# At the end of a turn px is added ahead of the gate and half a key unit follows the first turned rows; in the last turn unit 5 precedes the turned rows

## What is computed

```python
x = x + _L0_xattn_ref(ctx_1024, _layernorm(x), ...)   # selective scan over ctx, gated by silu of the normed x
x = x + _L0_ffn_ref(_layernorm(x), w1, w2)            # ternary-weight FFN, activations rounded to 8 bits
x = x + _L1_xattn_ref(_layernorm(x), ctx_1024, ...)   # cross attention, 16 heads, rms-normed q and k
x = x + _L1_ffn_ref(_layernorm(x), ...)               # mixture of 8 experts, top 2, and a shared one
```

```python
y = y + D[None, :, None] * u
y = y * jax.nn.silu(z)                                 # the gate
...
h = bitlinear(x, w1); h = new_gelu(h); h = bitlinear(h, w2)
...
k = rmsnorm((encoder_hidden_states @ Wk).reshape(B, Skv, H, D), gk)
return out.reshape(B, Sq, H * D) @ Wo
```

## Time and profile before

| | us |
|---|---|
| median of 3 runs | 1937.62 |
| lowest, highest | 1936.42, 1937.79 |
| profiled execution | 1934.49 |
| its span in the trace | 1932.8 |
| PE, DVE, ACT, POOL busy | 1797.8, 1206.4, 1090.6, 236.1 |

### The profile page before, as it was taken

How to read it: one execution, slowest core, us unless ns; L and a number is a source line. 1 busy time by engine, 2 the same in 40 slices (tenths; PEclk the granted TensorE clock), 3 DMA queues, 4 the chain that set the end, 5 groups by cost and what they waited for, 6 DMA issues and landing times.

```text
span 1932.8 us, 26062 instructions
## 1 busy us (share of the span) xinstructions
PE 1797.8 (93%) x8318; PEld 1154.4 (60%) x8319; DVE 1206.4 (62%) x1551; ACT 1090.6 (56%) x2454; POOL 236.1 (12%) x197
## 2 busy tenths in 40 slices
PE   7799899999999999999999999998989999989895
PEld 3455455776765576767655777765567676634442
DVE  5799778877775788777678977783641001144422
ACT  5577447666654676666547666754554554453420
POOL 0002011110100010000102000000031010033032
PEclk9799899999999989999999999999999999999997
DMA  7165222323231122223122323232044323213433
GB/s 213 44 191 189 88 57 66 93 76 94 83 84 61 51 87 89 91 77 102 50 88 66 93 76 103 76 120 77 33 137 90 78 68 85 49 50 108 127 105 124
DMA packets 113862, 175.76 MB, mean 91 GB/s; under 512 B 12400, under 2 KB 65648, under 8 KB 113280
## 3 DMA queue, kind: packets, MB, share of 16 engines
q1 hardware_dynamic: 99136, 158.06, 26.0%
q0 software_dynamic: 13840, 15.21, 3.9%
q10 hardware_dynamic: 816, 1.57, 0.2%
HBM read 146.23 MB, written 34.87 MB: 94 GB/s over the span
## 4 chain that ended last, share of the span: by engine, by line
PE 78%; DVE 9%; ACT 6%; issue 4%; another core or an unknown queue 2%; DMA 1%; POOL 1%; SPq 1%; ACTq 0%; DVEq 0%
PE ps L1942 27%; PE pp L1942 17%; PE px L1942 17%; PE pd L1942 6%; PE po L1942 5%; DVE arena L1469 2%; PE ps L2136 1%; PE pp L2290 1%; DVE arena L1461 1%; ACT hbuf L1235 1%; PE pd L2261 1%; PE po L2261 1%; ACT arena L980 1%; PE px L1994 1%
## 5 line engine op out<-in xcount | busy, mean ns | idle before, releaser
L1469 DVE TENSOR_TENSOR_SCAN arena<-arena 128x512 f32<-128x512 f32 x256 | 292.2, 1204 | 16.3 <-ACT arena L980 15.7
L1235 ACT ACTIVATE hbuf<-ps,shift,rms_k 128x512 f32<-128x512 f32 x256 | 198.4, 777 | 124.3 <-PE ps L1942 117.2
L1942 PE MATMUL ps<-qkT 128*128 128x512 f32 x512 | 250.8, 601 | 7.3 <-ACT hbuf L1235 4.0
L1942 PE MATMUL pp<-wq,xnT 128*128 128x256 f32 x1024 | 233.6, 382 | 0.0
L1942 PEld LDWEIGHTS pp<-wq,xnT 128*128 128x128 f32 x1024 | 191.6, 192 | 24.0
L813 POOL TENSOR_TENSOR rms<-ssv,minus_half 128x4 f32<-128x4 f32 x64 | 80.9, 1264 | 860.5 <-ACT ssv L1211 860.5
L980 ACT ACTIVATE arena<-arena,a_neg 128x512 f32<-128x512 f32 x256 | 163.7, 722 | 0.0
L1942 PEld LDWEIGHTS po<-v_ext,hbuf 128*128 128x128 f32 x768 | 105.9, 191 | 61.2 <-issue 61.2
L1942 PEld LDWEIGHTS ps<-qkT 128*128 128x128 f32 x512 | 82.5, 190 | 84.0 <-ACT hbuf L1235 58.2
L1461 DVE TENSOR_TENSOR arena<-arena,bc 128x2048 f32<-128x2048 f32 x56 | 126.3, 2287 | 6.7 <-issue 5.6
L1942 PE MATMUL px<-wo,oT 128*128 128x512 f32 x256 | 121.8, 596 | 5.9 <-issue 5.9
(11 more groups left out here) (340 smaller groups left out, 3034.2 us busy)
## 6 DMA issues: line engine op xcount, KB each, us to landing
bc<-bc_dram SPq DMA_DIRECT2D x56, 512.0 KB, 5.4
wo<-in_Wo SPq DMA_DIRECT2D x32, 512.0 KB, 3.6
wq<-in_Wq SPq DMA_DIRECT2D x32, 512.0 KB, 3.5
qkT<-kt_dram SPq DMA_DIRECT2D x32, 512.0 KB, 4.4
hbuf<-in_w SPq DMA_DIRECT2D x8, 1024.0 KB, 10.0
wv<-in_Wv SPq DMA_DIRECT2D x32, 256.0 KB, 2.8
kt_dram<-xnT SPq DMA_DIRECT2D x13, 512.0 KB, 3.0
wk<-in_Wk SPq DMA_DIRECT2D x25, 256.0 KB, 3.3
```

The costliest lines, as they stand in the source:

```text
L1235: nc.scalar.activation(pT[:, h, k], ps[s_use % 2][:], ACT.Exp, bias=shift[:, 0:1], scale=rms_k[:, bass.ds(G * (GH * NT) + (h * NT + k), 1) ...
L1469: V.tensor_tensor_scan(hb[i][:, e], dA[i][:, e], hb[i][:, e], 0.0, ALU.mult, ALU.add).then_inc(scan_done[i], 1)
L1942: return nc.tensor.matmul(out, lhsT, rhs, start=first, stop=last, **kw)
```

## The change

It moves work in four places and adds one instruction of ScalarE.

1. PE: at the end of turns 0 to 2 the first half of the next unit's k_turned goes from behind out_proj to behind `turned(7, 0)`. The wait for `o2_added` goes from ahead of scan_end to behind it (in the last turn to behind units 1 to 3).
2. VectorE: at the end of a turn the two px tiles are added ahead of gate_y instead of behind it.
3. ScalarE: in the last group of turns 0 to 2, ahead of the first `o_out`, a Silu of one column (`silu_of_eps`). The table of Silu is loaded there.
4. Last turn: PE runs `kss(4)` between the halves of ffn1(1), and unit 5's k_turned ahead of `ffn1_with_turned(2, 0)` instead of behind it. ScalarE takes kss(4) out ahead of gelu(1).

```diff
@@ ScalarE, FFN of a turn
                 gelu(0)
                 if not scan:
                     kt_out(4)
+                if not scan:
+                    for h in range(GH):
+                        kss_out(4, h)
                 gelu(1)
                 if scan:
                     scan_b(b + 1, turn_)
-                for h in range(GH):
-                    kss_out(1 if scan else 4, h)
+                    for h in range(GH):
+                        kss_out(1, h)
@@ ScalarE, last group
                     if is_last(g):
+                        if scan:
+                            nc.scalar.activation(silu_of_eps[:], eps[:], ACT.Silu)
                         o_out(G, 0)
@@ VectorE, last group
                     if is_last(g):
+                        for k in range(2):
+                            add_out(g, k)
                         if scan:
                             gate_y(b + 1)
-                        for k in range(NT):
+                        for k in range(2, NT):
                             add_out(g, k)
@@ PE, start of a turn
-                for i in range(2):
-                    pe.wait_ge(o2_added[i], b * NG + 1)
+                def o2_free():
+                    for i in range(2):
+                        pe.wait_ge(o2_added[i], b * NG + 1)
                 if scan:
                     scan_end(b, turn_)
+                    o2_free()
                     scan_a(b + 1, turn_, 0)
...
                         kss(i, 0)
+                    o2_free()
                 in_quant()
@@ PE, FFN of a turn
-                ffn1(1)
+                ffn1(1, range(0, 2))
+                if not scan:
+                    for h in range(GH):
+                        kss(4, h)
+                ffn1(1, range(2, HG))
                 if scan:
                     scan_b(b + 1, turn_)
                 for h in range(GH):
-                    kss(1 if scan else 4, h)
+                    if scan:
+                        kss(1, h)
+                    else:
+                        kt(5, h)
                 ffn1_with_turned(2, 0)
-                if not scan:
-                    kt(5, 0)
-                    kt(5, 1)
@@ PE, end of a turn
                 for_groups(pe, group)
+                if scan:
+                    n0 = unit_at(b + 1, 0)[0]
+                    k_turned(n0, b * NG + NG, b + B, 0)
                 for k in range(NT):
                     out_proj(NG - 1, k, range(1))
                 turned(NG - 1, 1)
                 for k in range(NT):
                     out_proj(NG - 1, k, range(1, GH))
                 if scan:
-                    n0 = unit_at(b + 1, 0)[0]
-                    for h in range(GH):
-                        k_turned(n0, b * NG + NG, b + B, h)
+                    k_turned(n0, b * NG + NG, b + B, 1)
```

More of the change, by code:

```diff
@@ L125, in program @@
         exp_of_eps = sb("exp_of_eps", [P, 1])
+        silu_of_eps = sb("silu_of_eps", [P, 1])
         conv_w = sb("conv_w", [P, EC, DC])
```

## The result

The changed kernel takes 1930.41 us (median of 6 runs, 1926.69 to 1931.07) against 1937.02 us (6 runs, 1935.16 to 1938.31) for the kernel before, run beside it: ratio 0.9965, 95% interval 0.9953 to 0.9977. That is 6.6 us faster, inside the predicted range of 1916 to 1931 and about half of the 13.6 us of the sum. The profiled execution took 1928.18 us, its span is 1926.5.

A forecast was written before the change was run, and what follows sets the result against it. TensorE (PE) was taken as the bound, on 78% of the chain. Turn-end waits 7.5, turn-end clock 3.4 and last turn's FFN 2.7 sum to 13.6 us: 1937.62 becomes 1924.0 us, range 1916 to 1931.

The forecast's parts named there:

- the sum: Whole kernel: turn-end waits 7.5, turn-end clock 3.4 and last turn's FFN 2.7 give 13.6 us saved.
- Waits at the turn ends: Ends of turns 0 to 2: scan_end starts 2.6, 2.5 and 2.4 us earlier, 7.5 us in all.
- rival (2): Turn ends: table load, dummy Silu or earlier adds keep the gate last; about 1.3 us less each, 1928; chance 0.07.
- Clock at the turn ends: From scan_end to in_quant, full clock returns: 1.0, 1.0 and 1.4 us, 3.4 in all, ends 0 and 5.4.
- The third term: Third turn end's clock: one of two half-rate stretches stays and takes 1.4 us, of 2.0 to 3.4 lost.
- Rival (1): Turn ends and last FFN: clock does not come back, only waits count, 7.6 us, 1930.0; chance 0.25.
- Last turn's FFN: Unit 5's k_turned fills the 3.32 us wait; ffn2(0) 3.8 us early, 2.7 us kept if the clock holds.
- I carry the saving over unchanged: Whole kernel: the 13.6 us saving is taken from the median 1937.62, giving 1924.0 us.
- rival (4): Turns 2 and 3 gain turn 1's half-rate stretches, 6.7 us each, with a 7.6 us gain: 1943.4; chance 0.08.
- rival (3): Turn 1's interior, moved in time, runs at full clock like turn 2: at most another 6.7 us, 1917.3; chance 0.13.

The follow-up runs named there:

- e2: Kernel before with only the last turn's FFN order changed, turn ends as before: 1915.81 us beside a before of 1913.53 us, ratio 1.0008.
- e6: Kernel before, unchanged, profiled a second time: 1937.98 us, one run.
- e9: Kernel before plus two filler matmuls of 512 columns in PE's wait ahead of xn_turned, every turn: 1933.42 us, ratio 0.9982 to before.
- e3: Changed kernel plus two filler matmuls of 512 columns in PE's wait ahead of xn_turned, every turn: 1897.59 us, ratio 0.9909 to before.
- e8: e7 plus scan_c's matmuls spread between and behind the quarters of ffn2(0) in turns 0 to 2: 1923.17 us, ratio 0.9939 to before.
- e11: e10 with scan_c's matmuls over 48 rows instead of 16, the 32 added weight rows zero: 1915.98 us, ratio 0.9894 to before.
- e4: Changed kernel plus two filler matmuls of 512 columns ahead of turn 2's first ffn1, where PE does not wait: 1900.79 us, ratio 0.9916 to before.
- e7: Changed kernel with late unit's k_sums half in xn_turned's wait, half between its transposes, plus one filler matmul: 1918.5 us, ratio 0.9905 to before.
- e10: The same kernel as e3 (changed kernel plus filler ahead of xn_turned), run in another set: 1919.73 us, ratio 0.9911 to before.
- e1: Kernel before with only the turn-end edits, last turn's FFN as before: 1906.06 us beside a before of 1913.53 us, ratio 0.9948.

## Why the prediction came out as it did

**Waits at the turn ends: right.** From the first turned rows to scan_end 2.75, 2.61 and 2.40 us against 2.6, 2.5 and 2.4. Of the third 0.4 us is clock: k_sums behind the old wait took 1.47 us and takes 1.05 now. The second wait for a copy stayed (0.73), the gate ended at 598.85, 0.8 us ahead of scan_end's start, and k_sums of the second half waits 0.48 where 0.5 was said. The loads lay in ACT's idle time, so rival (2) did not happen.

**Clock at the turn ends: right, a little small.** From scan_end to in_quant 1.03, 1.40 and 2.26 us came back against 1.0, 1.0 and 1.4. The third term is the one mis-sized: I kept one of the two half-rate stretches, and none stayed (1319 to 1329 reads 1.00). Rival (1) is refuted in its mechanism. The rule that led to it, the Trainium skill, TensorE: Matmul & The Clock Gate, section HAM oscillation, would have left the falls in place. With the waits of 1.3 to 1.4 us gone they went, at turn ends 0 and 1 in all ten profiles with the new order there, and the four with the old order (before, e2, e6, e9) keep them. In e3, e8 and e11 the third end does have one, with no wait over 0.5 us between out_proj and scan_end. So the clock can fall without a wait as long as the rule's, and removing the wait is not always enough. The edit takes the wait away and moves half of k_turned at once; no run does only one of the two, so which of them keeps the clock up is not shown.

**Last turn's FFN: right.** The turned rows start 1365.08 - 1343.83 = 21.25 us behind in_quant instead of 19.24: 2.0 later, 1.9 said. ffn2(0) is 3.8 us early, as said, and the work behind the FFN (xn_turned) 2.65 (2.7 said). PE in the timeline, after, with DVE's hidden_out(3):

```profile
1359.93 3.60 PE L1950 MATMUL pp<-ctx_att,arena 128*128 128x512 f32 x8
...
1365.08 1.09 PE L2144 MATMUL ps<-ident,qkT 128*128 128x128 f32 x8 [1.56 <-DVE qkT L1640]
...
1370.57 3.61 PE L1950 MATMUL px<-w2t,qk_raw 128*128 128x512 bf16 x15
...
1379.69 1.41 DVE L1628 SCALAR_TENSOR_TENSOR hbuf<-px,fsc,ws 128x512 f32<-128x512 f32 x2
```

The clock did not fall behind the shortened wait (1.56; 1.8 said).

**The step that failed: "I carry the saving over unchanged".** It assumed that all other stretches keep the clock that they had. Turn 2 did not: it lost 6.65 us around scan_c and xn_turned, and the last turn 1.67. The price stood in the prediction, 6.7 us for one turn, in rival (4). But that rival joined it to rival (1)'s smaller gain, "one alone gives 1936.7", and asked at which loss the sign turns. The case that happened, the forecast's own gains with one turn struck, was not priced. It gives 1924.0 + 6.7 = 1930.7, measured 1930.4, and that it fits so well is luck: the gains were 1.5 us larger than the sum, the losses 1.8 us larger than 6.7. The 6.7 itself was clock time and not time on the path: by the table the turn that fell in before took 5.4 us more than the one that did not, and of after's 3.4 + 5.1 = 8.5 us in turn 2, 6.65 lie on the path. That the time lies inside the range at all owes much to the range's upper end, which stood for rival (1), refuted above. Rows of before spoke for pricing that case: turns 1 and 2 run the same work, one lost 6.7 us of clock and the other none, so that the clock in a turn's interior was not a constant to carry over. I used this for rival (3), in the hopeful direction, with 0.13, and for rival (4), the other way, with 0.08. Turn 1 itself did not change (130.36 to 130.49).

What differs between turn 2 of before and of after is where it starts on the raster of the clock's changes: 0.06 and 0.87 of a step. The work from in_quant to scan_c is the same and as closely spaced (28.2 and 28.3 us). It repeats from execution to execution, a shift of 1.7 us changes it (e4), filling the wait lessens it (e3, e7, e10), and it is gone in e11. The trace of before alone has its three turns at 0.07, 0.24 and 0.06. It could have told that 3.8 us less at one end and 4.0 at the next put turn 2 at a place that no turn had shown, not that this place would be a bad one. Why a start there ends in a fall is open.

## What to carry to other kernels

Price a reordering in its own places from the waits and durations, as here, and then price separately that quiet stretches elsewhere (few-row or one-column matmuls, a wait between them) fall to half rate or recover; each is worth as much as an edit, and it has both signs. A kernel whose turn starts elsewhere on the clock's raster is another case, even where its code is the same. Then look at the granted clock of the whole span, not only where the code was edited: if the gain in place is whole and the total is not, a filler matmul in a remaining wait or more rows in a thin matmul may free it, at no cost where PE waits anyway. Judge variants by equal landmarks in the traces beside the medians, and look whether the falls lie at the same places on both sides.

## What the runs showed of the hardware

- Useless work made the bound engine faster: two matmuls (1.7 us) ahead of ffn1 shortened turn 2 from 131.64 to 128.56 us (e4), and two in a wait gained 3.9 us for the kernel before (e9).
- The half-rate stretches repeat in the same code from execution to execution, three times of three for the kernel after, to 0.05 us in stage times, with starts 4.2 us apart; yet a kernel whose turn 0 is the same instructions had falls there (e1, 128.06 instead of 125.06 us), with its in_quant at 0.045 on the raster of clock changes and those of the others at 0.050 or more.
- The place on that raster at which a turn starts sorts all 35 unchanged turns by their first fall: none from 0.05 to 0.14, just behind scan_c from there to 0.29, in scan_c from 0.87 over 0.98 to 0.045.
- A float32 matmul of 512 columns takes the same time over 48 rows as over 16 (3.88 us for scan_c's four).
- An early dummy activation costs 0.20 us, and the table load ahead of it 1.28 us, 1.30 us from the start of the load to that of the activation; ACT's next work had still to wait 1.15 us for PE.
